# Reordering the instruction streams of a cross-attention stage (third attention of a fused four-layer kernel)

## The reference, cut to what matters

```
def _L3_xattn_ref(x, context, ...):            # DIM 512, 16 heads of 32
    ctx_img, ctx_txt = context[:, :257], context[:, 257:]
    q     = rms_norm(linear(x, q_w, q_b), norm_q_w)
    k     = rms_norm(linear(ctx_txt, k_w, k_b), norm_k_w);  v     = linear(ctx_txt, v_w, v_b)
    k_img = rms_norm(linear(ctx_img, ...), norm_k_img_w);   v_img = linear(ctx_img, ...)
    out = attention(q, k_img, v_img) + attention(q, k, v)    # two softmaxes, summed
    return linear(out, o_w, o_b)
x = x + _L3_xattn_ref(_layernorm(x), ctx, ...)
x = x + _L3_ffn_ref(_layernorm(x), ...)        # weights as sign(w) * mean(|w|), rows in 8-bit groups of 64
```

## Time and profile before

| what | value |
|---|---|
| runs shown | 2728.17 us median of 3 (2728.02 to 2736.21) |
| the profiled execution | 2733.56 us, its span 2731.8 us |
| PE busy in the span | 2493.1 us (91%) |
| DVE, ACT, POOL busy | 1415.8, 807.9, 809.3 us |
| granted TensorE clock, mean | 0.941 of full speed |
| this stage's loop | from 2086.64 to 2500.87 us of the span |

### The profile page before, as it was taken

One profiled execution on the slowest core, in us unless ns is written; L12 is line 12 of the kernel. 1 busy time (PEld: TensorE's weight loads), 2 busy tenths in 40 slices (PEclk: granted clock), 3 DMA queues, 4 the chain that ended last, 5 costly groups with the idle time before them and its releaser, 6 DMA issues. The chain is left out here.

```text
span 2731.8 us, 31837 instructions
## 1 busy us (share of the span) xinstructions
PE 2493.1 (91%) x10738; PEld 1333.6 (49%) x10758; DVE 1415.8 (52%) x3511; ACT 807.9 (30%) x2106; POOL 809.3 (30%) x784
## 2 busy tenths in 40 slices
PE   7999999979799999999789898699988898896998
PEld 3455555544455655555555555344433444443444
DVE  4544442032211415666557676776643555557886
ACT  1134443122111114555420101311103455443232
POOL 2665553112100004221223333200003545453333
PEclk9999999989899999999679999899998899997999
DMA  6014000021385532110332123500012111101000
GB/s 176 1 73 161 15 19 1 0 81 44 100 286 189 201 124 68 45 39 14 107 121 93 69 104 137 202 6 4 8 30 83 46 46 47 39 26 37 9 8 10
DMA packets 86882, 195.80 MB, mean 72 GB/s; under 512 B 18378, under 2 KB 35178, under 8 KB 84430
## 3 DMA queue, kind: packets, MB, share of 16 engines
q1 hardware_dynamic: 80590, 180.79, 19.6%
q0 software_dynamic: 6144, 13.13, 1.7%
HBM read 150.32 MB, written 38.60 MB: 69 GB/s over the span
## 5 line engine op out<-in xcount | busy, mean ns | idle before, releaser
L3248 POOL TENSOR_SCALAR a_p<-a_p,a_li 100x257 f32<-100x257 f32 (+1 forms) x256 | 189.6, 762 | 135.3 <-DVE a_li L3125 135.3
L2879 PE MATMUL bank<-l_early,a_ctx 128*128 128x512 f32 (+1 forms) x384 | 186.1, 632 | 0.0
L633 POOL TENSOR_SCALAR a_shared<-a_shared,a_li 128x361 f32<-128x361 f32 x104 | 131.8, 1267 | 176.8 <-DVE a_li L538 176.8
L2314 PE MATMUL bank<-f_xT,s_w 128*128 128x400 f32 x512 | 180.8, 508 | 1.3 <-ACT f_xT L2338 1.3
L1940 PE MATMUL bank<-s_wgu,f_xT 128*128 128x512 f32 x384 | 168.9, 593 | 0.7 <-ACTq L2122 0.7
L2314 PEld LDWEIGHTS bank<-f_xT,s_w 128*128 128x128 f32 x512 | 98.9, 194 | 78.0 <-issue 5.6
L1661 POOL DMA_INDIRECT a_got<-slots_y,slots_of x32 | 34.5, 1078 | 292.7 <-POOLq L999 283.9
L1940 PEld LDWEIGHTS bank<-s_wgu,f_xT 128*128 128x128 f32 x384 | 72.7, 190 | 92.2 <-issue 90.5
L2879 PEld LDWEIGHTS bank<-l_early,a_ctx 128*128 128x128 f32 (+1 forms) x384 | 71.2, 195 | 93.2 <-issue 92.8
L2949 PE MATMUL bank<-ident,a_p 100*128 100x100 f32 (+1 forms) x384 | 52.7, 272 | 56.1 <-POOL a_p L3248 17.6
L335 PE MATMUL bank<-a_wk,a_ctx 128*128 128x512 f32 (+1 forms) x192 | 94.3, 612 | 7.0 <-DMA a_ctx<-in_ctxT 7.0
(11 more groups left out here) (448 smaller groups left out, 5173.8 us busy)
## 6 DMA issues: line engine op xcount, KB each, us to landing
f_triple<-in_L_ffn_triples SPq DMA_DIRECT2D x16, 768.0 KB, 4.1
rounded<-f_triple SPq DMA_DIRECT2D x16, 768.0 KB, 3.3
s_whole<-in_L_ffn_w SPq DMA_DIRECT2D x24, 512.0 KB, 3.5
e_wg<-in_L_ffn_w_gate SPq DMA_DIRECT2D x16, 704.0 KB, 4.7
e_wu<-in_L_ffn_w_up SPq DMA_DIRECT2D x16, 704.0 KB, 6.1
slots_x<-zero SPq DMA_DIRECT2D x4, 2304.0 KB, 16.4
e_xg<-slots_x SPq DMA_DIRECT2D x16, 512.0 KB, 5.3
e_wd<-in_L_ffn_w_down SPq DMA_DIRECT2D x16, 512.0 KB, 4.2
```

Source lines behind the costliest of these rows:

```text
L633: pool.tensor_scalar(p[s % NP], p[s % NP], li[:, b % 2, h:h + 1], None, ALU.mult).then_inc(normed, 1)
L2314: mm = nc.tensor.matmul(banks[f % 2][:, 0:GT], w[:, kc, f * P:(f + 1) * P], xT[:, kc, :], start=(kc == 0), stop=(kc == KC - 1))
L2879: mm = nc.tensor.matmul(bank[0:m, :], columns[:, kc], w[:, kc, :], start=(kc == 0), stop=(kc == KC - 1))
L3248: pool.tensor_scalar(p[g % 2][j][:, lo:hi], p[g % 2][j][:, lo:hi], li[:, h, i:i + 1], None, ALU.mult) \
```

## The change

Nothing is computed differently; instructions move within the streams of PE, DVE, ACT and POOL, and the ring's list follows. Two heads of the last group of the last image are scaled by DVE and not by POOL. The core of the diff:

```diff
 # ring list
-order += [[("k", n, 0)], [("k", n, 2)], [("v", n, 0)], [("v", n, 2)]][g]
+order += [[("k", n, 0)], [("k", n, 2)], [("q", n)], [("v", n, 2)]][g]
 order += [("t", b, GH * g + j) for j in range(GH)]
-order += [[("k", n, 1), ("x", n)], [("q", n)],
+order += [[("x", n), ("k", n, 1)], [("v", n, 0)],
           [("v", n, 1)] + [("kT", n, fb) ...] + [("qT", n)], []][g]
 # pieces of the last image, by group:  (3, 3, 2) -> (2, 2, 4); x0 turned after heads 2
 # PE, next image there
 turn_heads(b, 0)
+    turn_x(n)
     keys(n, 1)
-    turn_x(n)
 turn_heads(b, 1)
-    queries(n)
+    values(n, 0)
 scores(b, 3)
-    values(n, 0)
+    queries(n)
 turn_heads(b, 2); values(n, 1)
 # PE, end
+project_out(B - 1)
 totaled matmul
-project_out(B - 1)
 # DVE
 all_maxima(b, 1)
-inverses(b, 1)
 add_bias(n, 0)            # last image: + measure_first_tile()
 copy_heads(b, 0)
+inverses(b, 1)
 add_bias(n, 1)            # last image: add_output(b - 1), - measure_first_tile(), sum_pieces
 all_maxima(b, 2)
-inverses(b, 2)
 add_bias(n, 2)            # without the copy of the last key row
 copy_heads(b, 1)
+inverses(b, 2)
-add_query_bias(n)
+lay_last_key(n)           # that copy; last image: - round_first_tile()
 all_maxima(b, 3)
-mean_squares(n); inverses(b, 3)
+mean_key_squares(n); add_query_bias(n)
+                          # last image: inverses(b, 3); scale_last_heads(); round_first_tile()
 copy_heads(b, 2)
+mean_query_squares(n); inverses(b, 3)
 scale_keys(n); scale_queries(n); copy_keys(n)
 # end: sum_pieces of the last three pieces; add_output(B - 1); then the reading of the totals
 # DVE, new
+def scale_last_heads():
+    for j in range(2, GH):
+        dve.wait_ge(inverted, head(B - 1, G - 1, j) + 1)
+        for i, (lo, hi) in enumerate(HALVES):
+            ins = dve.tensor_scalar(p[1][j][:, lo:hi], p[1][j][:, lo:hi], li[:, GH * (G - 1) + j, i:i + 1], None, ALU.mult)
+        ins.then_inc(last_normed, 1)
 # POOL: root(b + 2) moves behind norm(b, 3); root_first_tile() before norm(b, 1) of the last image
 # ACT
 exponentials(b, 1); squares(n, 0)
-squares(n, 1)
 copy_x(n); signs(b, 0)
+squares(n, 1)
 exponentials(b, 2)
-squares(n, 2); query_squares(n)
 signs(b, 1)
+squares(n, 2); copy_values(n, 0)
 exponentials(b, 3)
-copy_values(n, 0)
+query_squares(n)
 copy_values(n, 1); copy_keys(n); copy_values(n, 2); exponentials(n, 0); signs(b, 2)
 # ACT, last image: sign x2; take_first_tile(); sign x2; round_rest()
```

More of the change, by code:

```diff
@@ L2778, in stage_L3_attention @@
             for g in range(3):
-                m = (3, 3, 2)[g] if b == B - 1 else 1 if i < 2 * PIECES else 0
+                m = (2, 2, 4)[g] if b == B - 1 else 1 if i < 2 * PIECES else 0
                 done[b, g] = list(range(i, i + m))
@@ L2799, in stage_L3_attention @@
                     order += [("o", b - 1)]
+                if not more and g == 2:
+                    order += [("x0",)]
         order += [("o", B - 1)]
@@ L2944, in turn_heads @@
                         h = GH * g + j
-                        pe.wait_ge(normed, head(b, g, j) + 1)
+                        if (b, g) == (B - 1, G - 1) and j >= 2:
+                            pe.wait_ge(last_normed, j - 1)
+                        else:
+                            pe.wait_ge(normed, head(b, g, j) + 1)
                         pe.wait_ge(*R.free("t", b, h))
@@ L3021, in _ @@
                         values(n, 1)
+                    else:
+                        turn_first_tile()
                     outputs(b, 2)
@@ L3082, in add_bias, with lay_last_key @@
                         .then_inc(R.empties("k", b, c), 1)
[L3083 to L3086, removed]
+                def lay_last_key(b):
+                    dve.wait_ge(*R.empty("k", b, 2))
+                    dve.wait_ge(k1_in, (b + 1) * 16)
+                    dve.tensor_copy(ks[0:1, 2, :], k1[:]).then_inc(k1_used, 1)
                 def add_query_bias(b):
@@ L3172, in _ @@
                 add_bias(0, 2)
+                lay_last_key(0)
                 measure(1)
@@ L3178, in _ @@
                 add_query_bias(0)
-                mean_squares(0)
+                mean_key_squares(0)
+                mean_query_squares(0)
                 dve.wait_ge(const, 4)
                 scale_keys(0)
+                scale_queries(0)
                 copy_keys(0)
@@ L3188, in _ @@
                     all_maxima(b, 1)
-                    inverses(b, 1)
                     if more:
                         add_bias(n, 0)
+                    else:
+                        measure_first_tile()
                     copy_heads(b, 0)
+                    inverses(b, 1)
                     if more:
@@ L3214, in _ @@
                     if more:
-                        mean_squares(n)
-                    inverses(b, 3)
+                        mean_key_squares(n)
+                        add_query_bias(n)
+                    else:
+                        inverses(b, 3)
+                        scale_last_heads()
+                        round_first_tile()
                     copy_heads(b, 2)
                     if more:
+                        mean_query_squares(n)
+                        inverses(b, 3)
                         scale_keys(n)
+                        scale_queries(n)
                         copy_keys(n)
                     else:
-                        sum_pieces(BOTH + 3, 5)
+                        sum_pieces(BOTH + 3, 2)
                     copy_heads(b, 3)
@@ L3232, in _ @@
                     take_output(b)
+                sum_pieces(BOTH + 5, 3)
+                add_output(B - 1)
                 dve.wait_ge(totaled, 1)
@@ L3243, in norm @@
                 def norm(b, g):
-                    for j in range(GH):
+                    for j in range(2 if (b, g) == (B - 1, G - 1) else GH):
                         h = GH * g + j
@@ L3276, in _ @@
                 root(0)
-                powers(0)
+                key_power(0)
+                query_power(0)
                 root(1)
@@ L3282, in _ @@
                 for b in range(B):
+                    if b + 1 == B:
+                        root_first_tile()
                     norm(b, 1)
@@ L3285, in _ @@
                         add_bias(b + 1)
-                    else:
-                        root_first_tile()
                     norm(b, 2)
                     if b + 1 < B:
-                        powers(b + 1)
+                        key_power(b + 1)
+                        query_power(b + 1)
+                    norm(b, 3)
                     if b + 2 < B:
                         root(b + 2)
-                    norm(b, 3)
                     if b + 1 < B:
@@ L3394, in _ @@
                         squares(n, 0)
-                        squares(n, 1)
                         copy_x(n)
                     signs(b, 0)
+                    if more:
+                        squares(n, 1)
                     exponentials(b, 2)
+                    signs(b, 1)
                     if more:
                         squares(n, 2)
-                        query_squares(n)
-                    signs(b, 1)
+                        copy_values(n, 0)
                     exponentials(b, 3)
                     if more:
-                        copy_values(n, 0)
+                        query_squares(n)
                         copy_values(n, 1)
@@ L3411, in _ @@
                         exponentials(n, 0)
-                    else:
-                        take_first_tile()
-                    signs(b, 2)
+                    if more:
+                        signs(b, 2)
+                for i in done[B - 1, 2][:2]:
+                    sign(i)
+                take_first_tile()
+                for i in done[B - 1, 2][2:]:
+                    sign(i)
                 round_rest()
```

16 lines of the change are left out of this document (6 added, 10 removed).

## The result

Median 2687.11 us over 4 runs (2679.81 to 2690.32), against 2732.19 over the 4 runs of the kernel before (2728.02 to 2736.77): ratio 0.9831, 95% interval 0.98 to 0.9861. It was forecast at 2678 (2664 to 2700), faster. The profiled execution, the slowest of the four, took 2690.32 us, its span 2688.5, mean granted clock 0.946.

A forecast was written before the change was run, and what follows sets the result against it. PE's stream (work, idle time, clock) was taken to bound the kernel. Images 0 to 6 give 47.6 us and the last 5.2, together 52.8; 50 was taken off 2728.17, giving 2678 (2664 to 2700).

The forecast's parts named there:

- The ring's reading of the wait in group 1: In group 1, DVE's bias standing behind the reciprocals, not POOL, was said to make the 2.34 us wait.
- rival 3: Waits of groups 1 and 2 are POOL's; only group 0 and the end gain: 2720 us, chance 0.05.
- Group 0: First head group of a pass: with the bias first, PE waits about 0.7 us for 1.28; gain 0.5.
- Group 1: Before heads 2 and 3, bias ahead of reciprocals: 2.8 us idle gained, plus 2.64 of clock if this wait drops it.
- Rival 1: Waits go, but the clock still falls once an image, since PE idles 0.7 in group 0: 2697 us, chance 0.12.
- Group 2: Queries ahead of heads 2, values 0 behind heads 1: wait 0.1 to 0.2 us for 2.03; gain 1.9.
- Group 3: DVE's key scaling ends at 31.7 us, PE comes to the keys at 32.1: 0.4 to spare, the thinnest margin.
- A pass: Steady images 2 to 6: 43.9 us, of it 42.34 work, waits 1.1, gaps 0.5, clock 1.00; 31.6 gained.
- the last image: To the FFN's first matmul, DVE's sums and rounding moved: last product starts at 39.6 us; gain 5.2, bounds 0 and 9.
- The sum: 47.6 us from images 0 to 6 plus 5.2 from the last image: 52.8; 50 taken off the median 2728.17.
- Rival 4: POOL's scaling bounds the pass: at 13 us a group, about 2760 us, slower; chance 0.04.
- Rival 2: DVE's four key scalings each wait for one POOL instruction: 3.3 us an image, 2701 us; chance 0.04.

The follow-up runs named there:

- kernel 1: The kernel before with DVE's key bias, then head copies, in front of the reciprocals in groups 0 and 1, images 0 to 6: 2704.85 us, ratio 0.9904.
- kernel 2: kernel 1 with ACT's weight piece of group 1 directly behind the exponentials and not behind the query squares: 2688.29 us, ratio 0.9843 to the kernel before.
- kernel 3: The changed kernel with queries and values 0 back in their old places on all engines: 2683.8 us, ratio 0.9843 to the kernel before.
- kernel 4: The changed kernel with ACT's weight piece of group 1 back in front of group 3's exponentials, swap kept: 2680.6 us, ratio 0.9816 to the kernel before.
- kernel 7: The changed kernel with two extra POOL tensor_tensor instructions ahead of the scaling of groups 1 to 3, images 0 to 6: 2684.14 us, ratio 0.9836.
- kernel 8: The changed kernel with four extra POOL tensor_tensor instructions ahead of the scaling of groups 1 to 3, images 0 to 6: 2701.41 us, ratio 0.9901.
- kernel 5: The changed kernel with reciprocals of groups 1, 2 and 3 back in front of the head copies, behind the bias: 2683.04 us, ratio 0.9833.
- kernel 6: The changed kernel with all edits for the last image (image 7) undone: 2681.51 us, ratio 0.9832 to the kernel before.

## Why the prediction was right, point by point

**What bounds.** Right: PE's stream, its idle time and its clock. The ring's reading of the wait in group 1 (DVE's bias, not the POOL that the row named) was tested by kernel 1 and holds; rival 3, which believed the row, was kernel 1's theory B and is out.

**Group 0.** Right in kind; 0.99 us of waits are left where I had 0.7, because both heads 2 and 3 are met late, one by the bias and one by POOL.

**Group 1.** Right: 3.01 went to 0.35 (0.2 forecast), and the query product to 3.68. That it was DVE's order that made the wait is half of the cause: image 6 of the kernel before has that order, no late exponentials and a wait of 1.18. But "if this wait is what drops it" was too simple. With this wait gone alone (kernel 1), the clock still fell once a pass, behind the 2.02 of group 2. Rival 1 had that mechanism; it did not come about only because the change cures both waits.

**Group 2.** The size was right (2.03 to 0.41, gain 1.6 for 1.9), the cause given was not the whole of it. I put it down to the swap, and of the pieces next to the exponentials I said only that they cost nothing and stand in nobody's way, with no gain for them in the sum. Kernels 2 to 4 show that either cures the wait: the swap is worth 0.11 where the piece has moved, the piece's place nothing where the swap is made. Nor did I look past image 3, where the product behind the wait of 2.03 runs at full speed (3.62); in image 4 of the kernel before it is a slow one:

```profile
2335.71 0.72 PE L2949 MATMUL bank<-ident,a_p 100*128 100x100 f32 x6 [2.03 <-ACT a_v L3322]
2336.27 5.32 PE L2879 MATMUL bank<-l_early,a_ctx 128*128 128x512 f32 x8
```

**Group 3.** Right: keys are scaled 0.96 before PE takes them up (2307.42 and 2308.38 in image 4). It is indeed the thin margin: it was the first thing to give way in kernel 7.

**A pass** was forecast at 43.9 and is 44.23: waits of 1.75 and not 1.1, gaps of 0.13 and not 0.5, two misses that partly cancel. Images 2 to 6 gave 29.9 (31.6 forecast), images 0 and 1 7.8 and 7.3 (8.0 each), the last image 3.6 (5.2). There the third maxima ended at t = 25.0 and not 24, and the reciprocals with DVE's scaling of two heads (1.73 of it the scaling) took 3.5 from there and not 2.7; the rounding won back 0.3 (4.4 for 4.7). So the last product started at 41.0 and not 39.6, and took 6.16 for 5.47. That the last image comes out near the forecast owes something to the clock: with the same instructions kernels 7 and 8 gained 7.9 and not 3.6, close to the bound of 9 that I gave for a product at full clock.

**The sum.** The stage gave 48.7 for 52.8. I took 50 off 2728.17, on the thought that the runs below the profiled one lacked the falls that the change removes. That correction did no good: the median over 4 runs of before is 2732.19, 4.0 higher, and the two medians differ by 45.1. So of the 9.1 us between 2678 and 2687.11, 4.0 lie in the base and 4.9 in the gain (0.2 is rounding), of which the stage explains 1.3. The other 3.6 lie outside the stage; in the profiled pair 5.4 were lost ahead of the loop, and I take them for the same scatter. How much of it there is the experiments show: kernels 4, 5 and 6, which by their traces are level with the changed kernel or behind it, have medians of 2680.6, 2683.04 and 2681.51, 4 to 6.5 below 2687.11, while the kernel before was only 1.6 to 2.7 lower beside them. A forecast that close to a median is therefore in part luck.

**Rival 4** (POOL as the bound) needed about 11 us of scaling a group to undo the gain; kernel 8, at 10 to 11 a group, lost 2.8 to 3.6 us a pass and kept more than half of it. Out for this kernel, and bounded too high in price. **Rival 2** did not happen in the changed kernel, whose key scaling became no longer (2.40 for three, 2.54 in the earlier trace rows); see the last section for where it does.

## What to carry to other kernels

In an in-order stream that shares a ring of banks, put the instruction that frees a bank ahead of those that wait for another engine; that alone was worth 3.8 us of a pass of 51.6, and 3.1 more went when a long independent piece stood behind one group's exponentials and no longer right in front of the next group's. When a wait for two semaphores names an engine that had long been done, follow the ring to the use three places back. And look at the clock beside every wait that is removed: a fall moves to the next long wait. PE's busy time in a pass went from 45.19 to 43.99 with the first wait gone and to 42.31 only with the second.

## What the runs showed of the hardware that was not expected

DVE's scaling of keys reads two SBUF tensors. Beside POOL's `tensor_scalar`, with one tensor input, three of them take 2.40 in the changed kernel, 0.07 longer than the 2.33 with POOL idle. Beside POOL's `tensor_tensor`, with two, they take 3.62 in kernels 7 and 8, and over the whole span of kernel 7 the median of one is 1410 ns:

```profile
L3111 DVE SCALAR_TENSOR_TENSOR a_k<-a_k,a_kr,a_nk x24: 730/1410/1412, 2078.8 to 2392.4; 128x512 f32<-128x512 f32 x16, 105x512 f32<-105x512 f32 x8
```

POOL's pair beside it took 2.67, and 2.15 where DVE did no such scaling (2301.51 and 2280.07 in kernel 7). The Trainium skill's page "SBUF — State Buffer", section "Who interferes with whom", lets such a DVE instruction exclude any GpSimd instruction that reads SBUF. These runs agree that the two contend where POOL's instruction has two inputs, but as a lengthening on both sides, and show next to none of it where it has one. POOL's two instructions differ also in width (512 and 257 columns) and its pair reads one tile twice; no run here separates that from the number of inputs. The edge decides about an engine's margin: 1.2 us here, more than the 0.96 to spare.
